# Weight loads on ScalarE's queue and the first batch's statistics ahead of the weight set-up, in both attention layers

## The reference

```python
x = x + _L0_gnn_ref(_layernorm(x), adj, W, a_src, a_dst, bias, ln_gamma, ln_beta)   # 4 heads of 64
x = x + _L0_ffn_ref(_layernorm(x), ...)                                             # state space block
x = x + _L1_gnn_ref(_layernorm(x), adj, W, a)                                       # 1 head of 256
x = x + _L1_ffn_ref(_layernorm(x), ...)                                             # LSTM and prefix sums
```

```python
dst = einsum('bhij,bhje->bhie', softmax(weight), h) + bias
out = relu(dst) + h
out = (out - mean) / sqrt(var + 1e-6) * ln_gamma + ln_beta
```

## Time and profile before

| what | value |
|---|---|
| time, median of 3 runs | 4492.12 us (4490.15 to 4494.11) |
| the profiled execution: its time | 4492.92 us |
| the profiled execution: span from first to last instruction | 4491.1 us |
| busy share of the span: PE, DVE, ACT, POOL | 89%, 77%, 64%, 26% |
| mean granted TensorE clock | 0.978 |
| first attention phase | 0 to 1017 us |
| second attention phase begins | 2417.6 us |
| LSTM phase begins | about 2960 us |

### The profile page before, as it was taken

One profiled execution on the slowest core, in us unless ns is written; L12 is line 12 of the kernel. 1 busy time (PEld: TensorE's weight loads), 2 busy tenths in 40 slices (PEclk: granted clock), 3 DMA queues, 4 the chain that ended last, 5 costly groups with the idle time before them and its releaser, 6 DMA issues. The chain is left out here.

```text
span 4491.1 us, 143052 instructions
## 1 busy us (share of the span) xinstructions
PE 3991.1 (89%) x55713; PEld 2858.3 (64%) x55713; DVE 3463.6 (77%) x9063; ACT 2881.7 (64%) x7050; POOL 1184.9 (26%) x1032
## 2 busy tenths in 40 slices
PE   7999999984999999999997999978888888888882
PEld 4666666652666666666665777767777777777772
DVE  6999999984888898889886888846666666666666
ACT  6999999973888888888885777733333333333330
POOL 4777777771222222222221111100000000000000
PEclk9999999997999999999998999999999999999996
DMA  2221222111000000000002433411211111111115
GB/s 66 71 68 65 76 76 74 60 57 57 20 29 29 20 29 29 29 20 29 29 20 72 142 132 133 143 41 33 44 34 41 37 42 36 41 37 42 36 39 161
DMA packets 326921, 251.57 MB, mean 56 GB/s; under 512 B 172136, under 2 KB 290664, under 8 KB 324200
## 3 DMA queue, kind: packets, MB, share of 16 engines
q1 hardware_dynamic: 324712, 234.00, 18.0%
q10 hardware_dynamic: 1536, 8.39, 0.5%
HBM read 157.87 MB, written 67.12 MB: 50 GB/s over the span
## 5 line engine op out<-in xcount | busy, mean ns | idle before, releaser
L2576 PE MATMUL lstm_G_psum<-next_Whh,lstm_HT 128*32 128x192 f32 x8192 | 440.3, 333 | 267.0 <-DVE lstm_HT L2706 266.4
L2647 ACT ACTIVATE lstm_TC<-lstm_G_psum 128x192 f32<-128x192 f32 x512 | 170.0, 332 | 708.3 <-PE lstm_G_psum L2576 708.3
L1540 ACT ACTIVATE ssm_EX<-ssm_Z_psum,ssm_tok 128x256 f32<-128x256 f32 (+1 forms) x1024 | 371.7, 423 | 156.0 <-PE ssm_Z_psum L1370 86.3
L2576 PEld LDWEIGHTS lstm_G_psum<-next_Whh,lstm_HT 128*32 128x32 f32 x8192 | 214.1, 109 | 354.0 <-DVE lstm_HT L2706 320.3
L2568 PE MATMUL lstm_G_psum<-next_Wih,lstm_XT 128*32 128x192 f32 x8192 | 428.6, 327 | 0.0
L2695 DVE SCALAR_TENSOR_TENSOR lstm_AB<-lstm_TC 128x128 f32<-128x128 f32 x512 | 149.9, 293 | 335.5 <-ACT lstm_TC L2647 331.4
L547 ACT ACTIVATE g_PR<-g_S,g_nmax 128x512 f32<-128x512 f32 x512 | 368.1, 722 | 1.5 <-DVE g_nmax L682 1.5
L689 DVE COPY g_PT<-g_PT_psum 128x512 f32<-128x512 f32 x512 | 344.4, 684 | 24.8 <-PE g_PT_psum L430 20.0
L538 ACT ACTIVATE g_relu<-g_Z_psum,g_src 128x512 f32<-128x512 f32 x512 | 346.5, 683 | 19.3 <-PE g_Z_psum L423 19.1
L2868 POOL TENSOR_SCALAR lstm_rstd<-lstm_mv 128x4 f32<-128x4 f32 x32 | 7.2, 226 | 1322.1 <-DVE lstm_mv L2689 1322.1
L682 DVE CUSTOM_DVE_ANT_0 g_S<-g_Z_psum,g_relu 128x512 f32<-128x512 f32 x512 | 345.7, 684 | 10.2 <-ACT g_relu L538 8.7
(11 more groups left out here) (313 smaller groups left out, 10883.7 us busy)
## 6 DMA issues: line engine op xcount, KB each, us to landing
g_ADJ<-in_adj SPq DMA_DIRECT2D x64, 1024.0 KB, 6.4
x<-g_XO SPq DMA_DIRECT2D x64, 512.0 KB, 5.3
g_X<-in_x SPq DMA_DIRECT2D x32, 512.0 KB, 4.3
ssm_X<-x SPq DMA_DIRECT2D x32, 512.0 KB, 3.9
x<-ssm_OUT SPq DMA_DIRECT2D x32, 512.0 KB, 2.9
g_X<-x SPq DMA_DIRECT2D x32, 512.0 KB, 4.3
lstm_U<-x SPq DMA_DIRECT2D x128, 128.0 KB, 3.5
lstm_V<-lstm_U SPq DMA_DIRECT2D x128, 128.0 KB, 3.3
```

What stands on the lines that cost most here:

```text
L1540: ins = act.activation(EX[h % NE][:, col:col + n], Zb[c][:, i * CHUNK:i * CHUNK + n], ACT.Exp, bias=tok[b.slot][:, i, c, h:h + 1])
L2576: ins = pe.matmul(bank[32 * j:32 * (j + 1), 0:last - first], HT[t % 2][:, 32 * kc:32 * (kc + 1)], Whh[:, kc, j, first:last], start=False, ...
```

## The change

In both attention phases the loads of W and `arow` are issued by ScalarE, as the first instructions of its program, in place of by SyncE. In both, VectorE takes the statistics of batch 0 right behind the two bf16 copies of constants, ahead of the copies that serve the weight set-up; they are no longer issued in the first `period`. In the first phase, bias, gamma and beta count on a semaphore of their own, `late`; TensorE and VectorE wait for `const` 32 (identity, pick4) and TensorE for `w` 64 (W, arow); GpSimd no longer waits for any table at its start, and waits for `late` 48 before the first `bias_added`. The diff, cut to its core:

```diff
@@ first_attention_phase: sync
             sp.dma_start(S[0][:, 0:H * P], consts["pick4"]).then_inc(s["const"], 16)
-            for kc in range(KC):
-                sp.dma_start(W[:, kc, :].rearrange("k (h e) -> k h e", h=H),
-                             weights["W"][:, kc * P:(kc + 1) * P, :].rearrange("h k e -> k h e")).then_inc(s["w"], 16)
-            sp.wait_ge(s["zero"], 1)
-            sp.dma_start(arow[0:20, :], weights["a_src"].rearrange("h t e -> (h t) e")).then_inc(s["w"], 16)
-            sp.dma_start(arow[32:52, :], weights["a_dst"].rearrange("h t e -> (h t) e")).then_inc(s["w"], 16)
-            for tile, name, sem in ((gamma, "gamma", "w"), (beta, "beta", "w"), (bias, "bias", "const")):
+            for tile, name in ((bias, "bias"), (gamma, "gamma"), (beta, "beta")):
                 sp.dma_start(tile[:, :], weights[name].rearrange("(o h) e -> o (h e)", o=1).to_broadcast([P, D])
-                             ).then_inc(s[sem], 16)
+                             ).then_inc(s["late"], 16)
...
@@ tensor
-            pe.wait_ge(s["const"], 48)
-            pe.wait_ge(s["w"], 6 * 16)
+            pe.wait_ge(s["const"], 32)
+            pe.wait_ge(s["w"], 4 * 16)
...
@@ scalar
+            for kc in range(KC):
+                act.dma_start(W[:, kc, :].rearrange("k (h e) -> k h e", h=H),
+                              weights["W"][:, kc * P:(kc + 1) * P, :].rearrange("h k e -> k h e")).then_inc(s["w"], 16)
+            act.wait_ge(s["zero"], 1)
+            act.dma_start(arow[0:20, :], weights["a_src"].rearrange("h t e -> (h t) e")).then_inc(s["w"], 16)
+            act.dma_start(arow[32:52, :], weights["a_dst"].rearrange("h t e -> (h t) e")).then_inc(s["w"], 16)
             act.wait_ge(s["v"], 1)
...
@@ vector (norm_stats itself is the same, only defined earlier)
-            v.wait_ge(s["const"], 48)
+            v.wait_ge(s["const"], 32)
             v.tensor_copy(ident_bf[:, :], ident[:, :]).then_inc(s["setup_v"], 1)
             v.tensor_copy(pick[:, :, :].rearrange("p h q -> p (h q)"), S[0][:, 0:H * P]).then_inc(s["setup_v"], 1)
+            norm_stats(Batch(None, 0, SLOTS))
             v.wait_ge(s["setup_pe"], 1)
...
-                at(b + 1, norm_stats)
+                if b.off >= 0:
+                    at(b + 1, norm_stats)
...
@@ gpsimd
             g.wait_ge(s["v"], 1)
-            g.wait_ge(s["const"], 48)
-            g.wait_ge(s["w"], 6 * 16)
...
             def bias_added(b):
+                if b.off == 0:
+                    g.wait_ge(s["late"], 48)
...
@@ second_attention_phase: sync
             sp.dma_start(scales[:, :], consts["row_scales"]).then_inc(s["const"], 16)
-            sp.dma_start(W[:, :, :], weights["W"].rearrange("(c k) e -> k c e", k=P)).then_inc(s["w"], 16)
-            for c in range(2):
-                sp.dma_start(arow[:, :, c], weights["a"][c * D:(c + 1) * D].rearrange("(k p) -> p k", p=P),
-                             allow_slow_non_contiguous=True).then_inc(s["w"], 16)
...
@@ scalar
+            act.dma_start(W[:, :, :], weights["W"].rearrange("(c k) e -> k c e", k=P)).then_inc(s["w"], 16)
+            for c in range(2):
+                act.dma_start(arow[:, :, c], weights["a"][c * D:(c + 1) * D].rearrange("(k p) -> p k", p=P),
+                              allow_slow_non_contiguous=True).then_inc(s["w"], 16)
...
@@ vector (the set-up copies move behind the definition of norm_stats)
+            v.wait_ge(s["const"], 48)
+            v.tensor_copy(ident_bf[:, :], ident[:, :])
+            v.tensor_copy(pick[:, :], S[0][:, 0:P]).then_inc(s["setup_v"], 1)
+            norm_stats(Batch(None, 0, SLOTS))
+            v.wait_ge(s["setup_pe"], 1)
...
-                at(b + 2, norm_stats)
+                if b.off > -2:
+                    at(b + 2, norm_stats)
```

More of the change, by code:

```diff
@@ L277, in first_attention_phase @@
         names = ("const w setup_pe setup_v adj_loaded mask st mv rs xn xt_pe xt h_pe h hb e_pe s1 s2 s3 s4 dst parts pt rows "
-                 "z relu s p t ev pv ot ob d1 d3 sum mean d4 sq ssq ln out rinv v zero check xb").split()
+                 "z relu s p t ev pv ot ob d1 d3 sum mean d4 sq ssq ln out rinv v zero late check xb").split()
         s = {n: m.sem(n) for n in names}
@@ L622, in _, with norm_stats @@
                 v.memset(rowsT[k][:, :], 0.0)
-            v.wait_ge(s["const"], 48)
+            def norm_stats(b):
+                b.dma_wait(v, x_loaded)
+                b.wait(v, s["xn"], IT, 0)
+                for t in range(IT):
+                    ins = v.bn_stats(stats[:, t, :], X[b.slot][:, t, :])
+                ins.then_inc(s["st"], 1)
+                b.wait(v, s["st"], 1, 1)
+                for t in range(IT):
+                    ins = v.bn_aggr(mv[:, t, :], stats[:, t, :])
+                ins.then_inc(s["mv"], 1)
+            v.wait_ge(s["const"], 32)
             v.tensor_copy(ident_bf[:, :], ident[:, :]).then_inc(s["setup_v"], 1)
             v.tensor_copy(pick[:, :, :].rearrange("p h q -> p (h q)"), S[0][:, 0:H * P]).then_inc(s["setup_v"], 1)
+            norm_stats(Batch(None, 0, SLOTS))
             v.wait_ge(s["setup_pe"], 1)
@@ L637, in _ @@
             ins.then_inc(s["setup_v"], 1)
[L639 to L648, removed]
             def make_mask(b, t):
@@ L2247, in _ @@
                 v.memset(rows[k][:, :], 0.0)
[L2248 to L2258, removed]
             def norm_stats(b):
@@ L2269, in norm_stats @@
                 ins.then_inc(s["mv"], 1)
+            v.wait_ge(s["const"], 48)
[3 more added lines that the diff above has]
+            v.wait_ge(s["setup_pe"], 1)
+            for e in range(KC):
+                v.tensor_copy(WT[:, e, :], Ab[e][:, 0:D]).then_inc(s["setup_v"], 1)
+            v.wait_ge(s["setup_pe"], 2)
+            for kc in range(KC):
+                v.tensor_copy(WA[:, kc, 0:3], Ab[2 + kc][:, 1:2].to_broadcast([P, 3]))
+                ins = v.tensor_copy(WA[:, kc, 3:4], Ab[2 + kc][:, 0:1])
+            ins.then_inc(s["setup_v"], 1)
             def make_mask(b, t):
```

## The result

| what | value |
|---|---|
| time after, median of 7 runs | 4477.16 us (4474.41 to 4478.77) |
| time before on the same chip, median of 7 runs | 4493.37 us (4490.03 to 4494.11) |
| ratio after to before, 95% interval | 0.9964 (0.9954 to 0.9974) |
| the profiled execution: span, time | 4474.9 us, 4476.79 us |
| both kernels again, with the later experiments | 4477.22 and 4492.72 us, ratio 0.9965 (0.9952 to 0.9979) |

The change takes 16.2 us off. 18.9 were forecast. The kernel before itself ran 1.25 us slower here than the 4492.12 from which the forecast started, so compare gains and not the bare times.

The account below looks back on a forecast made before the run. Two phase heads were taken as bound by an early wait for bias (first head) and by weight set-up serial with batch 0's statistics; gains 13.2 + 5.7 = 18.9 us, 4492.1 - 18.9 = 4473.2 us, range 4467 to 4481.

Parts of the forecast that it names:

- rival (a): First head: W and arow come late, batch 0 starts at 20.1, gain 8.85 us; about 4477.6 us; chance 0.12.
- Who gates the first head: First head: TensorE stands still 12.1 us until bias lands, which nobody needs this early; set-up and statistics needn't be serial.
- First head, the sum: First head: constants at 6.2, batch 0 on TensorE at 15.75 in place of 28.95, gain 13.2 us (12.0 to 14.4).
- the half microsecond for masks that hold the last normalising instruction: First head: masks starting about 14.3 may hold GpSimd's last instruction up to 1.06 us; half taken, 15.1 to 15.6.
- L780 and L2414: Both heads: masks keep GpSimd off; with masks later, 822 and 1216 ns fall to about 0.24 us.
- Slack of the set-up: First head: W and arow at 6.2, set-up ready at 14.3, 1.5 us ahead of batch 0's start at 15.75.
- Second head, the constants: Second head: const 0 to 1.3 us later, 0.3 taken; ScalarE normalises at 2426.8, gain 5.7 us (3.7 to 6.0).
- Carrying through: After the first head: nothing waits for something that doesn't move with it, so the shift is carried through the phase.
- rival (c): First layer: something unseen holds its pace, the 13.2 us return as a later wait; 4486.4 us; chance 0.06.
- TensorE's rate: First head: array at half rate until 45.10; slow work may cost up to 6.5 us or gain 4.5 us.
- rival (b): First head: TensorE's rise stays in absolute time, 4480 us, chance 0.07; or comes earlier, 4468.7 us, chance 0.04.
- Rival (d): Both heads: x lands late, moving statistics and set-up; kernel slower, at least 4501 us; chance 0.03.

Follow-up runs that it names:

- x_late_only: Kernel before plus only the separate signal for bias, gamma and beta, queues and order as before: 4487.77 us, one run (before in its group 4487.42).
- x_order_only: Kernel before plus only batch 0's statistics ahead of the weight set-up, in both heads: 4478.08 us, one run (before in its group 4487.42).
- x_act_later: Changed kernel, but ScalarE asks for W and arow only after VectorE's last fill of zeros, in both heads: 4482.29 us, ratio to before 0.9978.
- x_mask_shift: Kernel before; second head's first mask of batch 0 waits for GpSimd's scale and shift: 4491.63 us, one run (before in its group 4491.85).
- x_w_sp2: Changed kernel with W's load back on SyncE's queue in the second head only, arow staying on ScalarE's: 4477.41 us, one run.
- x_arow_sp2: Changed kernel with arow's two loads back on SyncE's queue in the second head only, W staying on ScalarE's: 4481.40 us, one run.
- x_sp_queue: Changed kernel with W and arow back on SyncE's queue in both heads, new order and signal kept: 4473.82 us, ratio to before 0.9959.

## Why the prediction was right, and where its terms were off

The time lay in the range and 4 us above the forecast, of which 1.25 are the slower kernel before. The gain was 2.7 us smaller than forecast, and 2.2 of these belong to the second head (3.5 for 5.7). The time alone is nearer to rival (a), at 4477.6; the rows decide against it, since TensorE's wait for batch 0 ends with GpSimd's work and not with the set-up. By its steps:

- **Who gates the first head.** Right. TensorE's 12.1 us until bias are gone, the first waits end with `pick` (6.93) and `arow` (7.52), and bias's own landing no longer matters to anybody. x_late_only and x_order_only show both halves of the argument separately.
- **First head, the sum.** 13.1 for 13.2, which is luck: two errors cancel. The constants were at 6.93, not 6.2 (0.7 late, inside the bounds), because W shares the engines with `pick`; with W asked for 1.1 us later they came at 5.75 (x_act_later). And the half microsecond for masks that hold the last normalising instruction was not paid: GpSimd's four took 4.85 us (4.84 in the earlier trace rows), while VectorE's three masks, which began at 15.27 when GpSimd was already in its last instruction, took 1.38 in place of 1.06. The one that came later waited, here VectorE. The Trainium skill ("SBUF — State Buffer", Who interferes with whom) says whoever issues first holds the other off, and both x_mask_shift and this row agree. It did not hold to the letter everywhere: in x_w_sp2 GpSimd's fourth instruction had been running for 0.7 us when the first mask began, and yet it was the one that took longer, 1.37 us in place of 1.22, while that mask took its usual 0.41. Batch 0 started 0.15 us later there by it.

```profile
14.76 1.37 POOL L785 TENSOR_SCALAR g_XN<-g_X,g_mv,g_rstd 128x256 f32<-128x256 f32 x1
...
15.46 0.41 DVE L654 TENSOR_SCALAR g_MASK<-g_ADJ 128x512 bf16<-128x512 int32 x1
```

- **L780 and L2414.** Right. In the groups of the changed kernel over the whole run (ns min/median/max) the outliers of the earlier trace rows are gone:

```profile
L780 POOL TENSOR_SCALAR g_rstd<-g_mv x32: 225/233/244, 9.4 to 921.8; 128x4 f32<-128x4 f32 x32
...
L2419 POOL TENSOR_SCALAR g_rstd<-g_mv x32: 225/225/238, 2413.9 to 2892.2; 128x4 f32<-128x4 f32 x32
```

- **Slack of the set-up.** Too generous. 1.5 us was the estimate, 0.34 the measurement: `arow` landed at 7.5, not at 5.5 to 6 (6.2 in the sum), and everything behind it followed in the durations foreseen. Rival (a), W and `arow` late, was given 0.12 and 20.1 us; it was nearer than that. In x_act_later the set-up does decide, at 20.98, for one microsecond of delay in asking.
- **Second head, the constants.** This is the term that was mis-sized: "Bounds 0 and 1.3 us later", with 0.3 taken. Measured were 2.6 us in one profile and 1.3 in the other. The upper bound was the moment at which everything had landed with one queue. That treats the loads as bytes that arrive by the same end in any order. But the constants are the last of SyncE's queue ahead of ADJ, and with half the engines' time given to ScalarE's queue all that stands before them is stretched. By x_arow_sp2, whose queues stand half and half too, that is worth about 1 us; the rest of the 2.6 has no cause shown. The other terms of that head were right: from the first cast to ScalarE's first normalisation are 4.28 us, where 4.4 were foreseen (2422.4 to 2426.8). With the loads on one queue the head gains 6.2 us, 0.2 above the forecast's upper bound of 6.0.
- **Carrying through.** Right. The span less the two heads is the same before and after (4447.3 and 4447.7 us), so rival (c) falls.
- **TensorE's rate.** The rise moved with the work, so rival (b) falls on both sides. Here are the changed kernel's counterparts of the earlier trace rows, 13.1 us earlier than those; the granted clock reads 1.00 from 28 to 34 us here, and from 41 to 47 before, so that column doesn't show this rise:

```profile
29.59 0.63 PE L416 MATMUL g_Z_psum<-g_rowsT,g_pick 128*128 128x512 bf16 x1
...
32.05 0.38 PE L416 MATMUL g_Z_psum<-g_rowsT,g_pick 128*128 128x512 bf16 x1
```

- **Rival (d).** x was never the last: in the first head it landed at 5.1 us (4.4 after it was asked for) and the statistics began at 7.41; in the second it landed 4.8 us after it was asked for, at 2409.3, and the statistics began at 2411.88.

## What to carry to other kernels

In a head, find for each consumer the landing of the last load it is made to wait for, and ask whether it reads that load: a table that nobody needs for 40 us held three engines here, and a signal of its own plus an order by need is worth 13.9 us in that head alone (x_sp_queue). Moving loads to another engine's queue gave nothing that was missing: the weights were asked for over a microsecond sooner and were in no sooner, and it cost 3.4 us, since the two queues share the same DMA engines and the small, urgent loads of the first came later. Put the urgent loads first on one queue. Asking for what is broadcast behind them all was tried only together with other changes of order, and gave no gain in time over one queue alone. If a second queue is used, look at its last small load: here a microsecond of delay in asking let it land 5.6 us later.

## What the runs showed of the hardware that was not expected

- A load of 5 KB, the last of a second queue, took 4.9 us when asked for at 2.60 us and 9.5 us when asked for at 3.56 us, beside the same loads of the first queue. On one queue, asked for at 3.83, it needed 3.4 us (landing seen at 7.19). Why is open.
- The spread of landings grows with two queues. First cast of the second head: 4.40 to 4.65 us in six profiles with one queue, 5.37 to 7.10 in five with two; of the changed kernel alone 7.10 and 5.77. The times of whole runs don't show this: x_act_later had 8.4 us between lowest and highest of 10 runs, but the kernel before, with one queue, had 9.6 in 14 runs beside it.
- Of a mask on VectorE and a GpSimd instruction already running, the mask was the one to wait in three profiles of four: the first mask took 0.71, 0.58 and 0.65 us (after, its second profile, x_arow_sp2), against 0.42 in x_act_later, where GpSimd was idle. In x_w_sp2 the mask took 0.41 and the running instruction 0.15 us more.
